# The third score unit of a causal attention loop: the 128-column row in front of the 384-column row

## The reference, cut to what matters

```python
# 16 sequences of 512 tokens, width 128; 16 heads of 64; 8 experts, hidden width 512
h = _layernorm(x, axis=-1) * (1 + ca) + sa
q = jnp.einsum('bsd,dhk->bshk', resid, W_Q)      # resid is h here
k = jnp.einsum('bsd,dhk->bshk', resid, W_K)
v = jnp.einsum('bsd,dhk->bshk', resid, W_V)
scores = jnp.einsum('bqhc,bshc->bhqs', q, k) / 8.0
scores = jnp.where(causal_mask, MASK_FILL, scores)
probs = jax.nn.softmax(scores, axis=-1)
z = jnp.einsum('bhqs,bshc->bqhc', probs, v)
out = jnp.einsum('bqhc,chd->bqd', z, W_out) + b_out
x = x + ga * out
h = _layernorm(x, axis=-1) * (1 + cb) + sb
x = x + gb * moe(h)       # router, best 2 of 8 experts, gelu, two matrices for each expert
```

## Time and profile before

| | us |
|---|---|
| median of 3 runs | 2003.7 |
| lowest, highest | 1998.6, 2003.99 |
| the profiled execution, its own time | 2000.88 |
| span in the profile | 1999.1 |
| PE busy | 1967.3 (98%) |
| VectorE busy | 1694.3 (85%) |
| ScalarE busy | 1581.1 (79%) |
| GpSimd busy | 745.2 (37%) |
| granted PE clock | 0.998 of full speed |

### The profile page before, as it was taken

How to read it: one execution, slowest core, us unless ns; L and a number is a source line. 1 busy time by engine, 2 the same in 40 slices (tenths; PEclk the granted TensorE clock), 3 DMA queues, 4 the chain that set the end, 5 groups by cost and what they waited for, 6 DMA issues and landing times.

```text
span 1999.1 us, 46357 instructions
## 1 busy us (share of the span) xinstructions
PE 1967.3 (98%) x12703; PEld 1538.2 (77%) x12703; DVE 1694.3 (85%) x4510; ACT 1581.1 (79%) x3765; POOL 745.2 (37%) x1222
## 2 busy tenths in 40 slices
PE   6999999999999999999999999999999999999998
PEld 4777777777777777777777777778888888888886
DVE  6887888888887888888888888989999998999997
ACT  6888888888888888888888888767777777777775
POOL 3444444444444444444444444322222222222222
PEclk9999999999999999999999999999999999999999
DMA  4100000000000000000000000212111111111120
GB/s 123 57 1 0 0 0 0 0 0 0 0 0 0 0 0 0 0 0 0 0 0 0 0 1 12 76 47 67 65 53 48 48 53 48 48 48 48 53 74 22
DMA packets 42252, 49.46 MB, mean 25 GB/s; under 512 B 3112, under 2 KB 24160, under 8 KB 42208
## 3 DMA queue, kind: packets, MB, share of 16 engines
q1 hardware_dynamic: 41952, 48.41, 7.6%
q0 software_dynamic: 256, 0.53, 0.1%
HBM read 44.47 MB, written 4.46 MB: 24 GB/s over the span
## 4 chain that ended last, share of the span: by engine, by line
PE 95%; DVE 2%; issue 1%; ACT 1%; POOL 0%; POOLq 0%; DMA 0%; DVEq 0%; SPq 0%; ACTq 0%
PE banks L543 15%; PE banks L558 15%; PE banks L517 13%; PE banks L618 6%; PE banks L620 6%; PE banks L619 5%; PE banks L639 5%; PE banks L637 5%; PE banks L638 5%; PE banks L465 4%; PE banks L467 4%; PE banks L466 4%; PE banks L580 1%; PE banks L582 1%; PE banks L581 1%
## 5 line engine op out<-in xcount | busy, mean ns | idle before, releaser
L438 POOL TENSOR_SCALAR probs<-probs,rdenom 128x512 f32<-128x512 f32 (+3 forms) x1024 | 522.3, 533 | 694.4 <-DVE rdenom L1079 694.4
L826 ACT ACTIVATE probs<-probs,neg_max 128x256 f32<-128x256 f32 (+3 forms) x1024 | 567.9, 555 | 71.7 <-DVE neg_max L1070 69.4
L1070 DVE CUSTOM_DVE_ANT_0 probs<-banks,mask_w 128x256 f32<-128x256 f32 (+3 forms) x1024 | 434.7, 480 | 82.0 <-PE banks L517 80.7
L917 ACT ACTIVATE hidden<-banks,b_cols 128x512 f32<-128x512 f32 x512 | 348.4, 685 | 195.6 <-PE banks L620 195.1
L1227 DVE TENSOR_TENSOR hid_lo<-hidden,hid_hi 128x512 fp32r<-128x512 f32 x512 | 380.9, 754 | 51.6 <-ACT hid_hi L925 37.9
L543 PE MATMUL banks<-ident,probs 128*128 128x128 f32 x2560 | 340.0, 275 | 3.1 <-POOL probs L438 2.1
L1063 DVE COPY probs_T<-banks 128x512 f32<-128x512 f32 x384 | 258.1, 686 | 88.3 <-PE banks L543 88.2
L418 POOL TENSOR_TENSOR acc<-acc,y_w 128x512 f32<-128x512 f32 x112 | 158.9, 1419 | 466.0 <-DVE y_w L1240 463.5
L543 PEld LDWEIGHTS banks<-ident,probs 128*128 128x128 f32 x2560 | 287.3, 140 | 47.8 <-DVE neg_max L1070 19.2
L558 PE MATMUL banks<-probs_T,v_sb 128*64 128x512 f32 (+3 forms) x2048 | 303.9, 439 | 0.2 <-DVE probs_T L1063 0.2
L558 PEld LDWEIGHTS banks<-probs_T,v_sb 128*64 128x64 f32 x2048 | 135.7, 136 | 146.8 <-issue 118.8
(11 more groups left out here) (139 smaller groups left out, 3374.1 us busy)
## 6 DMA issues: line engine op xcount, KB each, us to landing
w_rows<-w_kept SPq DMA_DIRECT2D x128, 256.0 KB, 3.8
x_all<-in_L_attn_resid_dram SPq DMA_DIRECT2D x16, 256.0 KB, 2.8
w_raw<-in_L_ffn_W_dram SPq DMA_DIRECT2D x16, 256.0 KB, 5.9
out_dram<-y_result SPq DMA_DIRECT2D x16, 256.0 KB, 2.3
v_sb<-in_L_attn_W_Q_dram SPq DMA_DIRECT2D x1, 512.0 KB, 6.3
v_sb<-in_L_attn_W_K_dram SPq DMA_DIRECT2D x1, 512.0 KB, 7.3
v_sb<-in_L_attn_W_V_dram SPq DMA_DIRECT2D x1, 512.0 KB, 9.4
v_sb<-in_L_attn_W_out_dram POOLq DMA_DIRECT2D x2, 256.0 KB, 6.8
```

Source lines behind the costliest of these rows:

```text
L438: pool.tensor_scalar(part, part, rdenom[:, p % 2, 4 * h + r:4 * h + r + 1], 1.0, ALU.mult, ALU.mult)\
L826: act.activation(part, part, ACT.Exp, bias=neg_max[:, p % 2, col:col + 1], scale=-1.0, accum_out=denom[:, p % 2, col:col + 1]).then_inc(p_ ...
L917: act.activation(hidden[:, e % 2, c, :], banks[:, c, :], ACT.Gelu, bias=b1_cols[:, e * HC + c:e * HC + c + 1]).then_inc(hid, 1)
L1070: dve.tensor_tensor_reduce(out=probs[:, p % 2, h, at:at + n], in0=S_BANK[u][h][:, col:col + n], in1=mask_w[:, 512 - n:512], scale=-SCALE, ...
```

## The change

In `scores`, the rows of a unit are walked in reversed order. Units 0 and 2 have a single row each, so only unit 1, the third in time, changes: its row 0 (128 columns) is computed first, its row 2 (384 columns) second. Banks, columns, operands, products and waits stay. The signal on `s_ps` stays on the unit's last matmul, which is now one of row 2. VectorE, ScalarE, GpSimd and SyncE have the same instructions in the same order.

```diff
-                        for r in UNITS[u]:
+                        for r in reversed(UNITS[u]):
                             n = (r + 1) * P
                             at = ROW_IN_BANK[r]
                             rows = slice(r * P, (r + 1) * P)
```

## The result

The changed kernel takes 2007.25 us (median of 14 runs, 2005.64 to 2009.29) against 2002.46 us (median of 14, 1998.6 to 2003.99) of the kernel before. The ratio is 1.0029, with a 95% interval of 1.0022 to 1.0035. It is not the quotient of the two medians, which lie 4.8 us or 0.24% apart. Slower it is; whether by more than the 0.3% that the prediction took as its bound isn't decided. The forecast was 2007.4 us, 5.1 us more than its base of 2002.3.

The account below looks back on a forecast made before the run. PE's own stream was taken as the bound: 128 x 0.045 = 5.8 us more, less 15 x 0.045 = 0.7 given back, is 5.1 us on a base of 2002.3, so 2007.4 us; range 2001.5 to 2013.0.

Parts of the forecast that it names:

- PE's stream is the bound: Attention steps: PE is held by its own work, 1213.25 of 1221.00 us, so its gain or loss counts 128 times.
- First short pair at no cost, second and third at 0.11: Third unit, 128-column pairs: the first hides its loads under a 512 pair, 0.06 us to the next start; the others 0.11.
- The first 384 pair stands 0.05 waiting: Third unit, row 2: its weight loads have only a short pair to hide under, so it waits 0.05 us.
- The change of shape costs the same behind a long stream: L517 to L558: the next load starts 0.07 us before the last pair's listed end, 0.265 to 0.27 after its start.
- 0.045 us in a step: Third unit: 0.945 us against 0.90, so 0.045 more per step, 128 x 0.045 = 5.8 us.
- 15 steps p = 2 give it back: PE's 16 transposes at p = 2: a 0.08 us wait for `z_done` shrinks by 0.045, 15 times, 0.7 us back.
- The signal on `s_ps` at no cost: End of the third unit: the signal comes 0.045 us later, within VectorE's 0.63 us of cover, so costs nothing.
- Rival A: L517 to L558: the long last pair costs 0.175 us, not 0.265; 5.7 us faster, 1996.6; chance 0.07.
- Rival C: L517 to L558: the last pair costs 0.33 us, not 0.265; 12.9 us slower, 2015.2; chance 0.11.
- Rival B: PE's steps: waits or the third short pair absorb the extra 0.045 us; within 1.5 us of before, 2002 to 2004; chance 0.09.
- The base: Whole kernel: starting time of 2002.3 us, the middle of the profiled 2000.9 and the three runs' median 2003.7.
- Theory 1: Third unit, the prediction's view: a short pair costs 0.11 us where a load follows, only its stream before the shape change.

## Why the prediction was right

Point by point, by its steps:

- *PE's stream is the bound.* Held. The steps p = 4 to 6 went from 9.22, 9.22 and 10.85 to 9.27, 9.27 and 10.90 us. One argument for it was weaker than it was put, that an engine which waits wouldn't repeat so exactly. The steps p = 2 do hold a wait, and 13 of 15 repeat at 10.91 to 10.93. And the nines of the clock row are coarse: the granted clock was 0.50 in 1304.4:1307.6 us. Neither touches the sum.
- *First short pair at no cost, second and third at 0.11.* Held: 0.06, 0.11, 0.11.
- *The first 384 pair stands 0.05 waiting.* Held: 388 ns, 385 forecast. The split of the short pair shows that the price doesn't go by the columns, and L604 that it goes by the load.
- *The change of shape costs the same behind a long stream.* Held, and this was the weakest step, argued from a pass of another kind. L558's load begins 453.72 - 453.46 = 0.26 us behind the last pair's start, 453.80 - 453.72 = 0.08 before its listed end. The Trainium skill says that a change of tiling mode drains TensorE, that is, lets the work under way run out ("TensorEngine Tiling (Array Packing)", Key Properties). The page gives no time; the trace agrees with the rule, for the load begins only 0.08 us before that end. The Trainium skill's other rule, that PE pulls weight loads ahead of matmuls in flight ("TensorE: Matmul & The Clock Gate", Part 2: What happens when you issue a matmul), does not reach over this change of shape: load and matmul both start at 453.72.
- *0.045 us in a step.* 0.047 at p = 4 to 6. The forecast of 5.1 us is for 128 steps; for the 124 of the whole stretch the same sum gives 124 x 0.045 - 0.7 = 4.9. Measured were 5.4. Of the 0.5 between them, 0.2 is the 0.047 in place of 0.045, and the next point has 0.05. The rest lies in the steps p = 3 and p = 7, which grew by 0.053 to 0.064 on average; why was not looked into.
- *15 steps p = 2 give it back.* Held for 14: their period didn't grow, and it grew by 0.05 once z_lo was early. The one of the last sequence has no wait to give, for its transposes take 1.91 us in the kernel before already; it grew from 10.85 to 10.90. The forecast wanted 1.95 us for the transposes, 1.94 came.
- *The signal on `s_ps` at no cost.* Held, 0.58 us of cover left.

Rival A (the long pair hides the change of shape) falls by the 0.26, where it wanted 0.175. Rival C (0.33) falls by the same number. Rival B (absorbed) holds for the steps p = 2 alone. The base was chosen well by some luck: 2002.3 was laid between two values, and 2002.46 is the median of more runs. That the medians lie 4.8 us apart, so near to 5.1, is partly luck too, since the rest of the program scatters by several us; the sound test is 5.4 against 4.9. And the chances were fair and not more: the ratio lies so near to 0.3% that "same" and "slower" were close to even.

## What to carry to other kernels

In these traces a pair of score matmuls costs the longer of two things, its stream and the next pair's weight loads (0.11 us for 128 weight columns). The last pair before the array changes its use costs its stream and then about 0.1 us. So a matmul too short to cover a weight load belongs last before such a change; how the others are ordered made 0.6 us in 1189. When an engine's period repeats to the hundredth, such a term can be read from the starts and multiplied by the count; look then for the few places with a wait, which take it in.

## What the hardware showed that was not expected

- A pair of 64-row matmuls of 64 columns costs as much as one of 128 columns where a weight load follows: 0.11 us. Splitting the last 384 columns into 256 and 128 costs only 0.01 to 0.02. Theory 1 had both figures ahead of the runs (0.11 and 0.012).
- PE's first rise to 2.4 GHz came 5 to 7 us apart between runs of the same kernel: before the scores of the first step began, or more than 3 us into them. The first step took 9.14 us or 10.4, with the same instructions.
- At the same wait of 3.0 us the clock fell to 1.2 GHz in 9 profiles of 13 and stayed up in 4. Falls like this one, and in two profiles a wait of 4.06 us at L610, go with the scatter of 761.8 to 768.1 us behind the last step's start.
- Compared by single profiles, the kernels would have shown 8.3 us of difference; from the fourth step to the last one they show 5.4, repeatable to 0.2.
